# A recommendation kernel: one more gathered column handed to ScalarE, and a re-cut last tile

## The reference

```python
emb = emb_tables[jnp.arange(26)[:, None], x_cat]           # 26 x 2048 rows of 64
emb = jnp.transpose(emb, (1, 0, 2))
dense_embed = price[:, None] @ Wp + bp
feats = jnp.concatenate([emb, dense_embed[:, None, :]], axis=1)
gram = jnp.einsum('bid,bjd->bij', feats, feats)
interactions = gram[:, _IU, _JU]                            # 27*26/2 = 351
h = jax.nn.relu(dense_embed @ W1 + b1)                      # 64 -> 128
dense_out = jax.nn.relu(h @ W2 + b2)                        # 128 -> 64
t = jax.nn.relu(jnp.concatenate([interactions, dense_out], axis=1) @ Wt1 + bt1)  # 415 -> 256
out = (t @ Wt2 + bt2)[:, 0]
```

## Time and profile before

| | |
|---|---|
| median of 3 runs | 525.37 us |
| the profiled execution | 526.02 us, of which the span of instructions is 524.1 us |
| GpSimd (POOL) busy | 381.8 us, 73% |
| TensorE (PE) busy | 251.3 us, 48% |
| ScalarE (ACT) busy, its DMA issues not counted | 165.6 us, 32% |
| VectorE (DVE) busy | 148.5 us, 28% |
| mean share of the 16 DMA engines for GpSimd's gathers | 30.7% |

### The profile page before, as it was taken

One profiled execution on the slowest core, in us unless ns is written; L12 is line 12 of the kernel. 1 busy time (PEld: TensorE's weight loads), 2 busy tenths in 40 slices (PEclk: granted clock), 3 DMA queues, 4 the chain that ended last, 5 costly groups with the idle time before them and its releaser, 6 DMA issues.

```text
span 524.1 us, 8045 instructions
## 1 busy us (share of the span) xinstructions
PE 251.3 (48%) x1496; PEld 183.4 (35%) x1496; DVE 148.5 (28%) x370; ACT 165.6 (32%) x405; POOL 381.8 (73%) x411
## 2 busy tenths in 40 slices
PE   0106234151469543443058772606246963467875
PEld 0105124051344323333053351605134333355764
DVE  6103304032240232314033132223324033143353
ACT  0023404133150342405024143332415016164463
POOL 6777777777777777777777777777777777777750
PEclk9999656565569766556566966665555888569798
DMA  6333333333333333233333333333332333332210
GB/s 192 27 28 29 28 29 27 29 28 28 28 29 27 29 28 30 28 28 28 28 30 27 28 29 28 29 29 29 27 29 28 27 30 28 28 29 26 28 22 2
DMA packets 17526, 16.50 MB, mean 31 GB/s; under 512 B 10530, under 2 KB 10786, under 8 KB 17347
## 3 DMA queue, kind: packets, MB, share of 16 engines
q0 software_dynamic: 12864, 13.20, 30.7%
q1 hardware_dynamic: 2884, 2.49, 1.5%
q10 hardware_dynamic: 1728, 0.30, 0.3%
HBM read 15.95 MB, written 0.01 MB: 30 GB/s over the span
## 4 chain that ended last, share of the span: by engine, by line
POOL 62%; issue 24%; PE 5%; DMA 3%; ACTq 2%; ACT 2%; DVE 0%; POOLq 0%
POOL gathered L251 61%; PE ps_mlp L571 3%; ACTq L171 2%; POOL pairs_of L251 2%; DMA gathered<-in_table,row_idx 2%; ACT gram L186 1%; PE ps_trans L500 1%; PE ps_gram L540 1%; DMA pairs_of<-in_table,row_idx 1%; PE ps_mlp L563 1%; ACTq L168 0%; DMA raw_idx<-in_x_cat 0%; POOLq L58 0%; ACT scores L344 0%; ACT top L339 0%
## 5 line engine op out<-in xcount | busy, mean ns | idle before, releaser
L251 POOL DMA_INDIRECT gathered<-in_table,row_idx x390 | 369.3, 947 | 120.4 <-issue 116.9
L540 PE MATMUL ps_gram<-feats 64*128 64x128 f32 x1024 | 111.9, 402 | 87.2 <-ACT gram L186 56.3
L540 PEld LDWEIGHTS ps_gram<-feats 64*128 64x128 f32 x1024 | 104.3, 306 | 101.5 <-issue 86.4
L186 DVE COPY gram<-ps_gram 32x112 f32<-32x112 f32 (+1 forms) x272 | 93.4, 343 | 152.8 <-PE ps_gram L540 149.6
L186 ACT COPY gram<-ps_gram 32x112 f32<-32x112 f32 (+1 forms) x272 | 93.7, 345 | 128.0 <-PE ps_gram L540 87.4
L500 PE MATMUL ps_trans<-ident,gathered 128*128 128x128 f32 x195 | 41.2, 368 | 173.9 <-DMA pairs_of<-in_table,row_idx 97.1
L500 PEld LDWEIGHTS ps_trans<-ident,gathered 128*128 128x128 f32 x195 | 31.0, 190 | 187.8 <-issue 186.3
L196 ACT COPY feats<-ps_trans 64x448 f32<-64x448 f32 (+1 forms) x60 | 34.1, 568 | 167.3 <-PE ps_trans L500 109.9
L196 DVE COPY feats<-ps_trans 64x448 f32<-64x448 f32 (+1 forms) x60 | 36.5, 609 | 148.9 <-PE ps_trans L500 148.3
L571 PE MATMUL ps_mlp<-gram,wt1p_sb 128*128 128x512 f32 (+2 forms) x168 | 60.8, 523 | 4.6 <-ACT gram L186 4.6
L571 PEld LDWEIGHTS ps_mlp<-gram,wt1p_sb 128*128 128x128 f32 x168 | 32.7, 229 | 33.7 <-issue 27.2
(11 more groups left out here) (31 smaller groups left out, 52.4 us busy)
## 6 DMA issues: line engine op xcount, KB each, us to landing
pairs_of<-in_table SPq DMA_DIRECT2D x1152, 0.2 KB
pairs_of<-in_table ACTq DMA_DIRECT2D x640, 0.2 KB
gathered<-in_table,row_idx POOLq DMA_INDIRECT x390, 3.3
price_bc<-in_price SPq DMA_DIRECT2D x1, 1024.0 KB, 7.1
wt1p_sb<-in_wt_pairs SPq DMA_DIRECT2D x1, 896.0 KB, 9.2
raw_idx<-in_x_cat SPq DMA_DIRECT2D x1, 195.0 KB, 2.6
pairs_of<-in_table,row_idx POOLq DMA_INDIRECT x12, 3.3
w_sb<-in_w ACTq DMA_DIRECT2D x2, 32.0 KB, 4.0
```

The costliest lines, as they stand in the source:

```text
L186: last = copy(gram_to[QUAD * c:QUAD * (c + 1), n % 2, t - BATCHES[n][0], :, rg * r:rg * (r + 1), :, s], source[QUAD * s:QUAD * (s + 1), :, ...
L251: pool.indirect_dma_start(out=field_at(t, f, 1), out_offset=None, in_=rows, in_offset=bass.IndirectOffsetOnAxis(ap=row_idx[:, at:at + 1], ...
L540: last = nc.tensor.matmul(ps_gram[:, out_at:out_at + P], group, group, start=True, stop=True)
```

## The change

- ScalarE fetches six columns (`ACT_TILES` = 2, 4, 6, 8, 10, 12) where it fetched five. It issues 32 rows after chunk 0's copies, 12 after chunk 1's, 12 after round 0's and 8 after round 1's: 64 per tile. A piece of more than 32 rows, or one that crosses a multiple of 128, is loaded in two.
- The batches are tiles 0-3, 4-7, 8-11, 12-13 and 14-15.
- The price network runs ahead: all of it is made in tiles 0 to 3, 512 samples in each, and `dense_out` is kept for all 2048.
- Tile 14 has four rounds of 16 matmul instructions in turn in two halves of `ps_gram`.
- The last tile goes in four units of 32 samples; a unit needs 6 columns of its own, and units 0 and 2 bring a seventh that they share with the next. Each unit is transposed, copied and multiplied by itself.
- The top layer of the last batch is made in two parts: 160 samples (tile 14 and unit 0), whose two output halves stand around unit 1's products, and the last 96 (units 1 to 3) at the end. Two DMAs write the scores.
- VectorE computes the row numbers of the last tile in 12 small additions where it made one; two index tables that GpSimd made go.

```diff
-UNITS = 2
-UNIT = HALF // UNITS
+UNITS = 4
+UNIT = P // UNITS
+SIDE = UNIT // 2
+COLS = FIELDS // UNITS
+SHARED = UNITS * COLS
 GROUPS = HALF // GROUP
...
+LATE = 3 * UNIT
+EARLY = 2 * P - LATE
+FINE_ROUNDS = UNITS
+FINE_RG = GROUPS // FINE_ROUNDS
+
+BATCHES = [(0, 4), (4, 8), (8, 12), (12, 14), (14, 16)]
+DENSE = BATCH // BANK
...
-ACT_TILES = (3, 6, 9, 12, 14)
+ACT_TILES = (2, 4, 6, 8, 10, 12)
...
-FIRST_ROWS, AFTER_FIRST_CHUNK, AFTER_CHUNKS, BETWEEN_ROUNDS = 24, 26, 10, 8
+FIRST_ROWS, AFTER_FIRST_CHUNK, AFTER_CHUNKS, AFTER_ROUND = 24, 32, 12, (12, 8)
...
+        def evacuate_unit(copy, n, kk):
+
+            src = ps_trans[D * kk:D * (kk + 1), BANK * (n % 2):BANK * (n % 2) + COLS // 2 * P]
+            src = src.rearrange("p (m q h b) -> p h m q b", m=COLS // 2, q=UNITS, h=2)
+            for h in range(2):
+                dst = feats[D * h:D * (h + 1), SIDE * n:SIDE * (n + 1), 1:1 + SHARED]
+                dst = dst.rearrange("p b (m k q) -> p k m q b", m=COLS // 2, k=2, q=UNITS)
+                last = copy(dst[:, kk], src[:, h])
...
+        def last_part(m, late):
+
+            if not late:
+                return slice(0, EARLY), ps_mlp[m][:, 0:EARLY]
+            return slice(EARLY, 2 * P), ps_trans[:, BANK * m:BANK * m + LATE]
...
-            sp.wait_ge(score_stored, len(BATCHES))
-            sp.dma_start(out.rearrange("(o b) -> o b", o=1), scores[:, :]).then_inc(out_written, 16)
-            sp.wait_ge(out_written, 16)
+            for late in range(2):
+                part = slice(BATCH - LATE, BATCH) if late else slice(0, BATCH - LATE)
+                sp.wait_ge(score_stored, len(BATCHES) + late)
+                sp.dma_start(out.rearrange("(o b) -> o b", o=1)[:, part], scores[:, part]).then_inc(out_written, 16)
+            sp.wait_ge(out_written, 16 * 2)
...
+            pool.wait_ge(rows_made, 2 + 3 * UNITS)
             pool.wait_ge(chunk_transposed[0], LAST)
-            for c, (f0, f1) in enumerate(LAST_CHUNKS):
-                if c == 1:
+            for n in range(UNITS):
+                if n == 2:
                     pool.wait_ge(chunk_transposed[1], LAST)
-                for f in range(f0, f1):
-                    gather(LAST, f, last_gathered[c])
+                for col in UNIT_COLS[n]:
+                    gather(LAST, col, unit_gathered[n])
...
-                    now = min(n, P - p0)
+                    now = min(n, P - p0, REGS)
...
             fetch_some(FIRST_ROWS)
             for t in range(LAST):
                 n = batch_of[t]
-                first = t == BATCHES[n][0]
+                first = t == BATCHES[n][0] and n > 0
                 odd_fields(0, t)
+                dense_slots(t)
+                if t < DENSE:
+                    dense_batch(t)
                 if first:
-                    dense_batch(n)
-                dense_slots(t)
-                if first and n > 0:
                     top_relu(n - 1)
                 fetch_some(AFTER_FIRST_CHUNK)
                 odd_fields(1, t)
-                if first and n > 0:
+                if t < DENSE:
+                    hidden_relu(t)
+                if first:
                     store_scores(n - 1)
                 fetch_some(AFTER_CHUNKS)
-                gram_round(0, t)
-                if first:
-                    hidden_relu(n)
-                fetch_some(BETWEEN_ROUNDS)
-                gram_round(1, t)
-                if first:
-                    dense_out_relu(n)
-
-            t, n = LAST, batch_of[LAST]
-            odd_last(0)
-            dense_batch(n)
+                for r in range(ROUNDS if t < LAST - 1 else FINE_ROUNDS):
+                    gram_round(r, t)
+                    if r < ROUNDS:
+                        fetch_some(AFTER_ROUND[r])
+                if t < DENSE:
+                    dense_out_relu(t)
+
+            t = LAST
             dense_slots(t)
-            top_relu(n - 1)
-            odd_last(1)
-            store_scores(n - 1)
-            hidden_relu(n)
-            dense_out_relu(n)
-            for r in range(LAST_ROUNDS // 2):
-                gram_round(r, t)
-            odd_last(2)
-            odd_last(3)
-            for r in range(LAST_ROUNDS // 2, LAST_ROUNDS):
-                gram_round(r, t)
-            top_relu(n)
-            store_scores(n)
+            odd_unit(0)
+            gram_round(0, t)
+            odd_unit(1)
+            part_relu(0)
+            gram_round(1, t)
+            odd_unit(2)
+            gram_round(2, t)
+            store_part(0)
+            odd_unit(3)
+            gram_round(3, t)
+            part_relu(1)
+            store_part(1)
...
+            for q in range(UNITS):
+                part = slice(UNIT * q, UNIT * (q + 1))
+                to = row_idx[part, b:e].rearrange("p (k c) -> p k c", c=PAIR)
+                from_ = clamped[part, b:e].rearrange("p (k c) -> p k c", c=PAIR)
+                base = field_base[part, 0:SHARED].rearrange("p (o g q) -> p q o g", o=1, q=UNITS)[:, q]
+                for c in (0, COLS + 1):
+                    nc.vector.tensor_tensor(to[:, :, c:c + COLS], from_[:, :, c:c + COLS],
+                                            base.to_broadcast([UNIT, 2, COLS]), ALU.add).then_inc(rows_made, 1)
+                nc.vector.tensor_tensor(to[:, :, COLS], from_[:, :, COLS],
+                                        field_base[part, SHARED + q % 2:SHARED + q % 2 + 1].to_broadcast([UNIT, 2]),
+                                        ALU.add).then_inc(rows_made, 1)
...
+            def top_part(m, late):
+
+                if not late:
+                    pe.wait_ge(score_stored, last_batch)
+                top_sums(last_batch, m, *last_part(m, late), rounds_before(LAST) + (FINE_ROUNDS if late else 1))
...
             for t in range(LAST):
                 n = batch_of[t]
-                first = t == BATCHES[n][0]
+                first = t == BATCHES[n][0] and n > 0
                 transpose_chunk(t, 0)
-                if first and n > 0:
+                if first:
                     top_layer(n - 1)
                 transpose_chunk(t, 1)
-                if first and n > 0:
+                if t < DENSE:
+                    hidden_layer(t)
+                if first:
                     score(n - 1)
-                gram_round(t, 0)
-                if first:
-                    hidden_layer(n)
-                gram_round(t, 1)
-                if first:
-                    dense_out_layer(n)
-
-            n = batch_of[LAST]
-            transpose_last(0)
-            top_layer(n - 1)
-            transpose_last(1)
-            score(n - 1)
-            hidden_layer(n)
-            dense_out_layer(n)
-            for r in range(LAST_ROUNDS // 2):
-                gram_last(r)
-            transpose_last(2)
-            transpose_last(3)
-            for r in range(LAST_ROUNDS // 2, LAST_ROUNDS):
-                gram_last(r)
-            top_layer(n)
-            score(n)
+                if t < LAST - 1:
+                    gram_round(t, 0)
+                    gram_round(t, 1)
+                else:
+                    for r in range(FINE_ROUNDS):
+                        fine_round(t, r)
+                if t < DENSE:
+                    dense_out_layer(t)
+
+            for n in range(UNITS):
+                transpose_unit(n)
+                if n == 1:
+                    top_part(0, 0)
+                fine_round(LAST, n)
+                if n == 1:
+                    top_part(1, 0)
+                if n == 2:
+                    score_part(0)
+            keep_warm(UNITS, 0)
+            for m in range(2):
+                top_part(m, 1)
+            score_part(1)
...
```

More of the change, by code:

```diff
@@ L345, in store_scores, with store_part @@
                                      ACT.Identity, bias=const(BT2, slice(0, 1))).then_inc(score_stored, 1)
+            def store_part(late):
+                part, _ = last_part(0, late)
+                first = BATCHES[last_batch][0] * P
+                act.wait_ge(score_summed, last_batch + 1 + late)
+                nc.scalar.activation(scores[:, first + part.start:first + part.stop],
+                                     ps_mlp[late][0:1, 0:part.stop - part.start],
+                                     ACT.Identity, bias=const(BT2, slice(0, 1))).then_inc(score_stored, 1)
             fetch_some(FIRST_ROWS)
@@ new lines, in top_sums @@
+            def top_sums(n, m, part, to, rounds):
+                a, first = BATCHES[n][0] * P, (n % 2) * SLABS * WIDE * P
+                nc.tensor.matmul(to, wt1d_sb[:, m * P:(m + 1) * P], dense_out[:, a + part.start:a + part.stop],
+                                 start=True, stop=False)
+                wait_gram_evac(rounds)
+                for j in range(SLABS):
+                    at = first + j * WIDE * P
+                    last = nc.tensor.matmul(to, wt1p_sb[:, j * TM1 + m * P:j * TM1 + (m + 1) * P],
```

(15 more changed lines are left out.)

232 lines of the change are left out of this document (123 added, 109 removed).

## The result

The changed kernel takes 524.27 us (median of 18 runs, 522.71 to 525.87) against 526.22 for the kernel before (median of 18 runs). The ratio is 0.9964, with a 95% interval of 0.9951 to 0.9978: 1.9 us faster, where 8.6 us slower was forecast. The profiled execution took 524.21 us, span 522.3.

A forecast was written before the change was run, and what follows sets the result against it. GpSimd's gather stream, one per 1.249 us, was taken as the bound, with ScalarE's room used up by fetches. 526.02 - 1.25 (gather) + 11.9 (waits) - 2.05 (end) = 534.6, so 534.0 against the median 525.37; range 521.3 to 541.5.

The forecast's parts named there:

- the price of the piece behind chunk 1's copies: ScalarE's time from chunk 1's copies to round 0's, with two rows more: 6.65 us in place of 5.97.
- The second load: Extra address load in odd tiles, where the piece behind chunk 1 crosses a multiple of 128: 0.5 us.
- the ledger of the forecast: Tile-by-tile sum of lateness of chunk 0's transposes against GpSimd's slack: 11.9 us of waits, tiles 6 to 10.
- The price network in tiles 1 to 3: Network work added to ScalarE's tile, half hidden behind TensorE: 2 us per tile.
- In tile 4 the top layer: Tile 4's period: 36.5 us plus 1.7 for top_layer waiting on tile 3's dense_out_relu, 38.2 in all.
- Rival 1: The fetches fit ScalarE's queue, 29.3 us per tile, GpSimd never waits: 522.1 us (521 to 525), chance 0.22.
- Rival 2: Partly: rows at 0.325 to 0.335 us, GpSimd waits of 3 to 8 us: 525 to 530, chance 0.18.
- The end: After the last gather: narrower top layer, one round's gram copies, more transposes and copies: -2.05 us, bounds -1.2 and -3.1.
- One gather fewer: GpSimd makes 401 gathers in place of 402 thanks to the sixth column: -1.25 us if it never waits.
- The start: Index tables and VectorE's 11 more additions ahead of ScalarE's first fetches: nothing, taken in by tile 0's wait.
- the fetch behind round 1: New piece of 8 rows behind round 1's copies: 4.74 us in place of 2.94; rival 1 has it filling a gap.
- The rule of the Trainium skill: Issuing on several engines saves only usually small DMA start time; by it the column would be cheap on ScalarE.

The follow-up runs named there:

- fill_after: The changed kernel with every row fetch of ScalarE and SyncE taken out, nothing in their place, fetched columns read as zeros, 401 gathers: 520.9 us, ratio 0.9911.
- fill_before: The kernel before with every row fetch of ScalarE and SyncE taken out likewise, 402 gathers: 525.7 us, ratio 1.0006 to the kernel before.
- fill_five: The changed kernel with ScalarE's columns and pieces of the kernel before, every row fetch taken out, 402 gathers: 522.15 us, ratio 0.9932.
- five: The changed kernel with the kernel before's five ScalarE columns in pieces of 26, 10 and 8 rows; ratios 1.0005, 1.0009, 1.0006 to the kernel before, in the condition.
- the 32 rows ahead of tile 0: The changed kernel with 32 rows instead of 24 fetched ahead of tile 0; ratios 0.9838, 0.9882, 0.9913 to the kernel before, in the condition.
- ten: The changed kernel with pieces of 32, 10, 12 and 10 rows, still 64 per tile; ratio 1.0031 to the kernel before, in the condition.
- before_24: The kernel before with pieces of 24, 12 and 8 rows instead of 26, 10 and 8; ratio 0.9996 to the kernel before, in the condition.

## Why the prediction was wrong

**What bounds the kernel, and the mechanism: right.** GpSimd's beat sets the time, ScalarE's queue fills up and passes its lateness to GpSimd over TensorE. In the trace after, chunk 0's copies stand behind fetches in tiles 5 to 11 and GpSimd waits at tiles 10 and 11, 2.8 us in all. The forecast had 11.9 us, at tiles 6 to 11. Taking all row fetches away (fill_after) takes the waits away.

**The step that failed is the price of the piece behind chunk 1's copies**, "5.97 + 2 x 0.34 = 6.65". It took 5.58 us in tile 6. The 5.97 holds a load of 10 addresses of 2.4 us, and it was carried over to the load of 12, as if its length came from the place. It comes from the start of that load, 2 past a multiple of 4; in the changed kernel every load starts at a multiple of 4, and 12 take 1.0. Rows 5 have 8 with 0.73 and 10 with 2.37, and I put the jump down to the copies in front. Two rows of the same trace, which the forecast did not use, have 12 and 10 addresses that start at a multiple of 4, behind chunk 0's copies of tiles 5 and 2:

```profile
L168 ACTq TENSOR_LOAD <-by_row_at x1: 951/951/951, 189.1 to 189.1; - x1
```
```profile
L168 ACTq TENSOR_LOAD <-by_row_at x1: 1272/1272/1272, 98.7 to 98.7; - x1
```

Measured from chunk 1's copies to round 0's are 5.48, 6.95, 5.23, 5.93, 5.58, 6.20 and 5.37 us in tiles 2 to 8 (in the odd ones with the second load, in tiles 2 and 3 with the network's `hidden_relu`), against 6.65 or 7.15 forecast: 7.3 us less over seven tiles. The second load was right at 0.5 (0.35 to 0.6 in tiles 5 and 7).

**What that step was worth.** With 5.6 in place of 6.65 and all else as forecast, the ledger of the forecast gives waits of 2.4 us in place of 11.9, at the first gathers of tiles 10 and 11 and nowhere else. The trace has 1.6 and 0.8 us there. So this one term carries the miss; but it is an account and not an experiment, as no run outside the condition had real row fetches and another load.

**Two smaller errors.** The price network in tiles 1 to 3 was forecast at 2 us per tile. From chunk 0's copies of one tile to the next pass 30.76 us in tile 2, 0.7 more than tile 6's 30.05, which is `dense_out_relu`. In tiles 1 and 3 it is 32.26 and 32.47, 1.3 to 1.9 more than in tiles 5 and 7 (30.57 and 30.98), which have the second load too. With this alone put right the ledger still gives 9.7 us. In tile 4 the top layer cost more than forecast, 39.4 us against 38.2: TensorE stood until `dense_out_relu` of tile 3 for 3.49 us, where the forecast had 1.7:

```profile
158.03 1.12 PE L627 MATMUL ps_mlp<-dense_out,wt1d_sb 64*128 64x512 f32 x2 [3.49 <-ACT dense_out L363]
```

With the load and the network put right the ledger gives 0.7 us, with tile 4's 39.4 us as well 2.9; the trace has 2.8. From chunk 0 of tile 1 to chunk 0 of tile 11 passed 321.6 us (59.8 to 381.4), forecast 332.3.

**The term that broke the forecast is a difference of large numbers.** A tile is 31.1 us for GpSimd and was 31.1 to 31.6 for ScalarE; 1 us in the second moved the sum by 9. The ledger's own range, for the row's price and small choices, was 4 to 20 us of waits, and 2.8 lies outside it. That 524.3 lay in the stated range is due to the chances given to rivals 1 and 2, not to the ledger.

**The end** was put at -2.05 with bounds of -1.2 and -3.1, and gave -4.0 in the trace and -3.6 between the medians of fill_before and fill_five. The copies of one round in place of two gave their 2.2 us (2.12 against 4.29). What I missed is the clock. I priced the top layer by its width, and the first 14 matmuls at 2.83 us were slow ones of that execution; now the clock is 1.00 in that stretch, and both halves take 1.8. At the full clock the old end took 17.6 us (fill_before) and not 18.2, and the new one 14.2 to 14.9.

**One gather fewer**, -1.25: right (fill_after against fill_five). The start was put at nothing and was 0.7 us longer up to the ninth gather; why stays open.

**Rival 1** (the fetches fit, 521 to 525) has the time in its range, but by luck: its reason, that the fetch behind round 1 fills a gap, is false (4.75 us, as forecast), a tile cost ScalarE 30.05 us and not 29.3, and GpSimd did wait. Rival 2 (small waits of 3 to 8 us, 525 to 530) had nearly the mechanism that came, with an end 2 us shorter. A row did cost 0.33 us in its sense (10.54 / 32 in tile 6), but the three pieces other than the one behind chunk 1 came out as forecast, so the row's price is not what moved the sum.

**The rule of the Trainium skill** (DMA: Bandwidth & Descriptors, Issuing engines are not separate DMA queues), that issuing elsewhere saves only a small issue time, led nearer to the time, as by it the second rival's sum (525 to 530) was to come, but by accident. This case does not bear it out for a column fetched row by row: the issue of 128 rows is 43 us of ScalarE's queue, and the runs price the fetches of the changed kernel at 2.8 to 3.4 us in all against 1.25 saved.

**Does the sixth column pay?** By the runs it does not: 520.9 without its cost, 524.27 with it, and 522.15 with five columns and no fetches, which cost nothing at 44 per tile in the kernel before. That five columns with the new end would take about 522.3 us with real fetches, 2 us less than the changed kernel, is argued from these and not measured; five, five_b and five_c ran in the condition alone. The same holds for the 32 rows ahead of tile 0.

## What to carry to other kernels

When work is moved from the engine that sets the time to one with room, add up the receiver's own cycle, piece by piece, at the size each piece will have, and where two rows of one instruction differ more than their sizes do, look for a third row before one of them is used. If the two cycles come out within 2% of each other, the sign of the change is open, and the text should say so. And measure the two halves of a change apart: here the end gave 3.6 to 4.0 us, the column saved 1.25, and the fetches took about 3 back.

## What the runs showed of the hardware

- On ScalarE's queue a load of row addresses into registers (TENSOR_LOAD) took 0.48 to 0.61 us for 4, 0.72 to 0.80 for 8, 0.95 to 1.02 for 12, 1.7 for 24 and 2.1 to 2.3 for 32 addresses, when start and count were multiples of 4. From such a start 10 took 1.2 to 1.3 and 26 took 2.1. From a start 2 past a multiple of 4, the only other kind in these runs, 10 took 2.3 to 2.4 and 12 took 2.8 (before, after, ten, before_24).
- A chip can be in a condition in which SyncE issues row DMAs at 0.4 per us in place of 3.4 while GpSimd gathers, and the kernel before takes 864 to 878 us in place of 526. What brings it about stays open. It was not there when the result was measured, with row fetches in both kernels; in the experiments it was there in each of the four batches whose kernels fetched rows and in neither of the two whose kernels did not, though the kernel before, which does, ran in all of them. One of ten runs of fill_before took 1066 us, which stays open too.
- Without the eight filler matmuls TensorE stood idle 2.12 us, its granted clock was 0.50 behind that (1.2 GHz), and the 28 matmuls there took 3.0 us more than at 1.00 (cold). Behind 2.8 to 3.0 us idle with the old end, 28 matmuls took 3.6, 4.9 or 5.0 us, from one execution to another.
